# A fused graph-attention and expert-routing block on one core: an expert tile's transposed rows copied on ScalarE, the norms' small sums on GpSimd, new engine orders

## The reference

```python
x = x + gnn(layernorm(x), adj)      # 4-head graph attention, masked softmax over 128 neighbours
h = layernorm(x)
h1 = h + causal_attention(rmsnorm(h, ln1_w)) @ wo.T        # 4 heads, 2 key/value heads, rotary
flat = rmsnorm(h1, ln2_w)
probs = softmax(flat @ router_w.T);  tp, ti = top_k(probs, 2)    # 8 experts
out = sum over e of weights[:, e] * ((silu(flat @ w1[e].T) * (flat @ w3[e].T)) @ w2[e].T)   # hidden 341
x = x + h1 + out
```

## Time and profile before

| | before |
|---|---|
| median of 3 executions | 1731.81 us (1727.41 to 1735.3) |
| the profiled execution | 1738.94 us, span 1737.1 |
| PE busy | 1524.0 us, 88% of the span |
| DVE busy | 1409.4 us, 81% |
| ACT busy | 1052.2 us, 61% |
| POOL busy | 913.5 us, 53% |
| granted PE clock, mean | 0.976 |

### The profile page before, as it was taken

How to read it: one execution, slowest core, us unless ns; L and a number is a source line. 1 busy time by engine, 2 the same in 40 slices (tenths; PEclk the granted TensorE clock), 3 DMA queues, 4 the chain that set the end, 5 groups by cost and what they waited for, 6 DMA issues and landing times. The chain is left out here.

```text
span 1737.1 us, 40737 instructions
## 1 busy us (share of the span) xinstructions
PE 1524.0 (88%) x10930; PEld 1122.8 (65%) x10930; DVE 1409.4 (81%) x4725; ACT 1052.2 (61%) x4092; POOL 913.5 (53%) x720
## 2 busy tenths in 40 slices
PE   4778998999899899999999999999999899987672
PEld 3555666776676667766667676777676666765451
DVE  4678888898889888988898888888889888875441
ACT  3576666766666667666666666666666666653221
POOL 2134565555555555556656655556555555555433
PEclk8899999999999999999999999999999999999897
...
DMA packets 141737, 79.08 MB, mean 46 GB/s; under 512 B 31909, under 2 KB 137165, under 8 KB 141261
## 3 DMA queue, kind: packets, MB, share of 16 engines
...
...
## 5 line engine op out<-in xcount | busy, mean ns | idle before, releaser
L452 POOL DMA_INDIRECT out<-ys,xt x264 | 430.5, 1631 | 511.5 <-DMA out<-ys,xt 383.4
L436 POOL DMA_INDIRECT routed<-fx,slot x256 | 257.9, 1007 | 199.1 <-DVE slot L845 131.7
L1132 PE MATMUL bank<-w_s,hsT 128*128 (+1 forms) x1584 | 230.3, 282 | 17.2 <-ACT hsT L599 16.5
L1132 PEld LDWEIGHTS bank<-w_s,hsT 128*128 128x128 f32 (+1 forms) x1584 | 202.8, 192 | 65.7 <-issue 60.9
L592 ACT ACTIVATE sg<-bank 128x341 f32<-128x341 f32 x264 | 120.6, 457 | 165.0 <-PE bank L1111 149.3
L541 ACT ACTIVATE p<-ub,nm 128x128 f32<-128x128 f32 x512 | 198.0, 390 | 34.3 <-DVE nm L767 33.7
L1111 PE MATMUL bank<-w_s,xT 128*128 x528 | 203.0, 466 | 6.6 <-DVE xT L907 3.0
L598 ACT ACTIVATE hsT<-bank 128x256 f32<-128x256 f32 x264 | 101.2, 384 | 165.7 <-PE bank L1125 141.1
L913 DVE SCALAR_TENSOR_TENSOR hg<-sg,bank 128x341 f32<-128x341 f32 x264 | 133.7, 507 | 82.8 <-ACT sg L592 77.1
L1115 PE MATMUL bank<-w_s,xT 128*128 x528 | 197.0, 455 | 0.1
L1125 PE MATMUL bank<-ident,hu 128*128 128x128 f32 (+1 forms) x792 | 137.6, 283 | 54.1 <-DVE ys L931 43.0
...
## 6 DMA issues: line engine op xcount, KB each, us to landing
xt<-routed SPq DMA_DIRECT2D x264, 65.0 KB
...
out<-ys,xt POOLq DMA_INDIRECT x264
...
```

The lines of the kernel that those rows point to most:

```text
L436: pool.indirect_dma_start(routed, bass.IndirectOffsetOnAxis(slot[p][:, i:i + 1], 0), fx[i // GB][p][:, i % GB, :], None).then_inc(S[f"sc{p ...
L452: pool.indirect_dma_start(out_rows, bass.IndirectOffsetOnAxis(xt[r][:, C:C + 1].bitcast(I32), 0), ys[r][:], None, compute_op=ALU.add, **bo ...
L1132: last = pe.matmul(y_p[:, 0:C], hsT[r % 2][0:n, c, :], w2_s[0:n, bass.ds(e, 1), c, :].rearrange("p a c -> p (a c)"), start=c == 0, stop=c ...
```

## The change

Three things are changed.

1. The copy of the transposed tile from PSUM to xT is done by ACT in place of DVE, with the same waits and the same semaphore. The step E.x moves from the lists of DVE to those of ACT.
2. The small sums in front of the three roots are done by POOL, directly before its root. DVE's step T.ms is gone; N.nx and M.na end on DVE with the statistics.
3. ORDER is laid out anew for PE, DVE, ACT, POOL and SP. In FILLING and DRAINING E.x and T.ms leave DVE's lists, E.x joins ACT's, and the rest keeps its sequence, PE's included.

The ORDER table and the moved steps:

```diff
 ORDER = {
     "pe": """
-        F.x.7 T.yT F.t.6 G.xn F.u.7 G.h F.d.6 A.hN G.p1.0 A.q E.x.0 F.t.7 G.p1.1 E.u.0 T.wo F.d.7 E.x.1 A.k G.o1.0 E.u.1 E.t.0 G.p1.2 E.x.2
-        E.d.0 G.v1.0 E.u.2 E.t.1 T.f A.s2.0 E.d.1 E.x.3 T.lg E.t.2 E.u.3 G.o1.1 E.d.2 A.s2.1 T.rank G.v1.1 E.x.4 A.o2.0 G.o1.2 E.u.4 G.p1.3
-        G.v1.2 E.t.3 E.x.5 A.s2.2 E.d.3 A.v2.0 E.t.4 E.u.5 G.o1.3 A.o2.1 A.s2.3 A.v2.1 G.v1.3 A.o2.2 E.x.6 G.ot E.d.4 A.v2.2 E.u.6 E.t.5
+        F.x.7 T.yT G.xn F.u.7 G.h F.t.6 A.hN G.p1.0 F.d.6 A.q E.x.0 T.wo F.t.7 E.u.0 G.o1.0 F.d.7 E.x.1 G.p1.1 E.u.1 E.t.0 A.k G.v1.0 E.d.0
+        G.p1.2 E.x.2 T.f E.t.1 E.u.2 A.s2.0 E.d.1 E.x.3 T.lg E.t.2 G.o1.1 E.u.3 A.o2.0 E.d.2 A.s2.1 T.rank G.v1.1 A.v2.0 E.x.4 G.o1.2 E.u.4
+        G.p1.3 G.v1.2 E.t.3 E.x.5 A.s2.2 E.d.3 E.u.5 A.o2.1 E.t.4 G.o1.3 A.s2.3 A.v2.1 G.v1.3 A.o2.2 G.ot E.d.4 E.x.6 A.v2.2 E.t.5 E.u.6
         A.o2.3 E.d.5 A.v2.3""".split(),
     "dve": """
-        G.xn F.x.7 A.hN T.yT F.d.6 F.u.7 F.g.7 G.p1.0 E.x.0 A.q E.u.0 T.wo E.g.0 E.x.1 F.d.7 G.p1.1 T.ms E.u.1 A.kk E.g.1 E.x.2 T.f E.d.0
-        G.p1.2 E.u.2 A.s2.0 E.d.1 E.g.2 E.x.3 T.lg E.u.3 E.d.2 E.g.3 E.x.4 T.rank A.s2.1 E.u.4 E.g.4 G.p1.3 E.x.5 A.s2.2 E.d.3 T.tab N.nx
-        E.u.5 A.s2.3 E.x.6 G.ot E.d.4 E.g.5 A.rb E.u.6 M.na E.g.6 E.d.5""".split(),
+        G.xn T.yT A.hN F.u.7 F.g.7 G.p1.0 F.d.6 A.q E.u.0 T.wo E.g.0 F.d.7 G.p1.1 E.u.1 T.f E.g.1 A.kk E.d.0 G.p1.2 E.u.2 E.g.2 A.s2.0 E.d.1
+        T.lg E.d.2 E.u.3 E.g.3 A.s2.1 T.rank E.u.4 E.g.4 G.p1.3 A.s2.2 N.nx E.d.3 T.tab A.s2.3 E.u.5 G.ot E.g.5 E.d.4 A.rb M.na E.u.6 E.d.5
+        E.g.6""".split(),
     "act": """
-        G.xn F.u.7 F.t.6 G.h A.hN F.t.7 E.u.0 A.v G.p1.0 T.wo E.u.1 G.o1.0 E.t.0 G.p1.1 A.kk E.u.2 E.t.1 T.f G.v1.0 A.s2.0 E.t.2 E.u.3 T.lg
-        G.p1.2 G.o1.1 G.v1.1 G.o1.2 E.u.4 A.s2.1 A.o2.0 E.t.3 T.rank G.v1.2 G.p1.3 A.v2.0 A.s2.2 E.u.5 A.o2.1 G.o1.3 A.v2.1 G.v1.3 E.t.4
-        A.o2.2 A.s2.3 A.v2.2 E.u.6 E.t.5 A.o2.3 A.v2.3""".split(),
+        F.x.7 G.xn F.u.7 G.h F.t.6 A.hN E.x.0 G.p1.0 F.t.7 E.u.0 A.v G.o1.0 E.x.1 T.wo E.u.1 E.t.0 A.kk G.p1.1 E.x.2 E.t.1 E.u.2 T.f E.x.3
+        G.v1.0 A.s2.0 E.t.2 G.o1.1 T.lg A.o2.0 E.u.3 G.p1.2 G.v1.1 E.x.4 E.u.4 G.o1.2 A.s2.1 E.t.3 E.x.5 A.v2.0 G.v1.2 G.p1.3 A.s2.2 E.u.5
+        A.o2.1 G.o1.3 A.v2.1 G.v1.3 E.t.4 A.o2.2 A.s2.3 T.rank E.x.6 A.v2.2 E.t.5 E.u.6 A.o2.3 A.v2.3""".split(),
     "pool": """
-        F.s.6 F.s.7 T.ms E.s.0 E.s.1 T.sc.0 E.s.2 T.sc.1 E.s.3 T.sc.2 T.sc.3 N.nx T.sc.4 G.ot T.sc.5 T.sc.6 M.na T.sc.7 E.s.4 E.s.5""".split(),
+        F.s.6 T.ms F.s.7 E.s.0 E.s.1 E.s.2 T.sc.0 T.sc.1 T.sc.2 N.nx T.sc.3 T.sc.4 E.s.3 G.ot T.sc.5 T.sc.6 M.na T.sc.7 E.s.4 E.s.5""".split(),
     "sp": """
-        F.l.7 E.l.0 E.l.1 E.l.2 E.l.3 E.l.4 E.l.5 N.nx T.f E.l.6""".split(),
+        F.l.7 E.l.0 E.l.1 E.l.2 E.l.3 E.l.4 N.nx E.l.5 T.f E.l.6""".split(),
 }
...
     # POOL, step ms_ (nx and na get theirs in the same way)
+                    pool.wait_ge(S["sq"], t + 1)
+                    pool.tensor_scalar(ve_t[:], ms[:], 1.0 / C, EPS_RMS, ALU.mult, ALU.add).then_inc(S["ve_t"], 1)
                     pool.wait_ge(S["ve_t"], t + 1)
                     pool.tensor_tensor(r3[:], ve_t[:], half[:, 0, :], ALU.pow).then_inc(S["r3"], 1)
...
     # ACT
+                def out_x(r):
+                    act.wait_ge(S["xtr"], k8 + r + 1)
+                    if late(k8, 1) or r >= 2:
+                        act.wait_ge(S["h3"], k8 + r - 1)
+                    act.activation(xT[r % 2][:], x_p[:, 0:128], ACT.Copy).then_inc(S["xT"], 1)
...
     # DVE
-                def out_x(r):
-                    dve.wait_ge(S["xtr"], k8 + r + 1)
-                    if late(k8, 1) or r >= 2:
-                        dve.wait_ge(S["h3"], k8 + r - 1)
-                    dve.tensor_copy(xT[r % 2][:], x_p[:, 0:128]).then_inc(S["xT"], 1)
```

More of the change, by code:

```diff
@@ L61 @@
     "dve": """
[L62 to L64 removed]
+        G.xn A.hN F.u.7 F.d.6 F.g.7 N.nx T.yT G.p1.0 A.q E.u.0 T.wo E.g.0 F.d.7 G.p1.1 E.u.1 A.kk E.g.1 E.d.0 T.f A.s2.0 G.p1.2 E.u.2 E.d.1
+        E.g.2 T.lg E.u.3 A.s2.1 E.g.3 T.rank E.d.2 E.u.4 G.p1.3 E.g.4 A.s2.2 E.d.3 T.tab E.u.5 A.s2.3 E.g.5 G.ot E.d.4 A.rb E.u.6 E.g.6 M.na
+        E.d.5""".split(),
     "act": """
[L66 to L68 removed]
+        F.x.7 F.t.6 F.u.7 G.xn G.h A.hN G.p1.0 E.x.0 E.u.0 F.t.7 A.v T.wo E.t.0 E.x.1 E.u.1 A.kk G.o1.0 G.p1.1 E.t.1 E.x.2 E.u.2 T.f G.v1.0
+        A.s2.0 E.x.3 E.u.3 T.lg G.o1.1 E.t.2 G.p1.2 G.v1.1 A.o2.0 E.x.4 A.s2.1 E.u.4 G.o1.2 E.t.3 E.x.5 A.v2.0 G.v1.2 G.p1.3 A.s2.2 A.o2.1
+        G.o1.3 E.u.5 E.t.4 A.v2.1 G.v1.3 A.s2.3 A.o2.2 E.x.6 E.u.6 A.v2.2 E.t.5 A.o2.3 T.rank A.v2.3""".split(),
     "pool": """
@@ L401, in nx @@
                         pool.wait_ge(S["xn"], 4 * n)
+                    pool.wait_ge(S["mv_g"], 4 * n + 4)
+                    pool.tensor_scalar(ve_g[:], mv_g[:, :, 1], EPS_LN, None, ALU.add).then_inc(S["ve_g"], 1)
                     pool.wait_ge(S["ve_g"], n + 1)
@@ L405, in na @@
                 def na():
-                    pool.wait_ge(S["va"], a + 1)
+                    pool.wait_ge(S["mv_a"], 4 * a + 4)
                     if late(a, 1):
                         pool.wait_ge(S["hN"], 4 * a)
+                    v = mv_a[:, :, 1]
+                    pool.tensor_scalar(va[:, 0, :], v, EPS_LN, None, ALU.add)
+                    pool.tensor_scalar(va[:, 1, :], v, 1.0 + EPS_RMS, EPS_RMS * EPS_LN, ALU.mult, ALU.add).then_inc(S["va"], 1)
+                    pool.wait_ge(S["va"], a + 1)
                     pool.tensor_tensor(rr[:], va[:], half[:], ALU.pow).then_inc(S["norm_a"], 1)
@@ L601, in steps @@
                 return {"xn": xn_, "hN": hN_, "h": h, "v": v, "kk": kk_, "wo": wo_, "f": f_, "lg": lg_, "rank": rank, "v1": values1, "v2": values2,
-                        "p1": exp1, "s2": exp2, "o1": out1, "o2": out2, "u": gate, "t": out_h}
+                        "p1": exp1, "s2": exp2, "o1": out1, "o2": out2, "x": out_x, "u": gate, "t": out_h}
             act.wait_ge(S["ready"], 2)
@@ L706, in wo_ @@
                                       z[p][:].rearrange("p b c -> p (b c)"), ALU.add).then_inc(S["x2"], 1)
-                def ms_():
-                    dve.wait_ge(S["sq"], t + 1)
-                    if late(t, 1):
-                        dve.wait_ge(S["r3"], t)
-                    dve.tensor_scalar(ve_t[:], ms[:], 1.0 / C, EPS_RMS, ALU.mult, ALU.add).then_inc(S["ve_t"], 1)
                 def f_():
@@ L931, in weigh @@
                         dve.tensor_scalar(ys[r][:], y_p[:, 0:C], xt[r][:, C + 1:C + 2], None, ALU.mult).then_inc(S["ys"], 1)
-                return {"nx": nx, "na": na, "xn": xn_, "hN": hN_, "wo": wo_, "ms": ms_, "f": f_, "q": q_, "kk": kk_, "lg": route1,
-                        "rank": route2, "tab": tab, "p1": scores1, "s2": max2, "ot": ot, "rb": rb, "yT": yT_, "x": out_x, "u": gate, "g": gated, "d": weigh}
+                return {"nx": nx, "na": na, "xn": xn_, "hN": hN_, "wo": wo_, "f": f_, "q": q_, "kk": kk_, "lg": route1,
+                        "rank": route2, "tab": tab, "p1": scores1, "s2": max2, "ot": ot, "rb": rb, "yT": yT_, "u": gate, "g": gated, "d": weigh}
             steps(-1, 1)["nx"]()
```

18 lines of the change are left out of this document (6 added, 12 removed).

## The result

The changed kernel takes 1715.24 us (median of 4, 1713.48 to 1718.73) where the kernel before took 1731.32 (4 runs, 1727.41 to 1735.3) in the same comparison: a ratio of 0.9906 with a 95% interval of 0.9883 to 0.9929. It is 16 us faster, where 39 were forecast. The profiled execution took 1714.39 us with a span of 1712.6, against 1738.94 and 1737.1.

A forecast was written before the change was run, and what follows sets the result against it. PE was taken as nearest bound, about 46.2 us of a 49.56 us body. Per body 1.6 + 0.33 - 0.25 - 0.3 = 1.4, taken as 1.6; 24.5 x 1.6 = 39 us less, 1693 against the median; range 1670 to 1730.

The forecast's parts named there:

- Bodies of 48.0 us: 24.5 x 1.6 = 39 us less: Sum over the ORDER bodies: each 1.6 us shorter, taken from 1.4 to 2.5, giving 39 us in all.
- the ogT wait: PE's output transposes wait for ACT's last copy, about 1.0 us per body, unexplained; left in, gain about 2.5 if it goes.
- the 46.19 that was read as the floor: PE's busy time per 49.56 us body: no order of the same matmuls could go under about 46.2 us.
- The wait of 1.6 us at E.t.1: PE waits for tile 0's weighing on DVE, behind scalings awaiting a late POOL root; 1.6 us per body would go.
- Fill and drain: I cost both at nothing, bounds -8 and +4: Both ends of the kernel: PE's order unchanged, the drain set by POOL's landing chain; cost nothing, bounds -8 and +4 us.
- rival C: Slower because xT is late on ACT: 0.4 us PE wait per copy, 1.6 us per body, 1771 us; chance 0.09.
- What changes is the queue that it stands in: xT copy: behind score operations on DVE, about 2.1 us; behind four exponentials on ACT, 1.56 us; cost nothing except two places.
- Rival D: Slower by small sums on POOL at 1.04 us each: POOL's floor up 3, body 1 us longer, 1756 us; chance 0.05.
- Rival A: POOL becomes the bound, bodies end at 48.9 us: only 16 us less, 1716 us; chance 0.17.
- POOL's floor: Shortest body POOL allows, from scatter landings plus its other work: 46.6 to 49.2 us, where it was about 45.6.
- Rival B, nothing gained,: The 1.6 us per body turn up again at another in-order wait: 1732 us; chance 0.10.
- Rival E: The unexplained wait for ACT's last attention output copy goes too: 2.5 us per body, 61 less, 1671 us; chance 0.07.

The follow-up runs named there:

- chip M: Chip of a later comparison: the unmodified changed kernel took 1721.25 us there, ratio 0.9888 to the kernel before, which took 1742.02 us.
- chip N: Chip of the last comparison, both kernels unmodified: the changed kernel took 1756.06 us, ratio 1.0084 to the kernel before.
- moves_only: Kernel before with xT copied on ACT, each E.x right ahead of its E.u, and small sums on POOL, but the old ORDER: 1897.8 us, ratio 1.0928.
- ends_dve: Changed kernel with the copy of xT back on DVE in FILLING and DRAINING only: 1705.37 us, ratio 0.982 to the kernel before.
- order_wide: Changed kernel with ORDER serving bodies 4 to 31, so also 4, 5 and 31: 1702.99 us on chip K, 1703.95 on chip M.
- xt_alone: Kernel before with only the xT copy moved to ACT, each E.x right ahead of its E.u: 1900.36 us, ratio 1.094.
- sums_alone: Kernel before with only the four small sums moved to POOL, old order otherwise: 1779.08 us, ratio 1.0229.
- pool_plus_again: Changed kernel with one more unread 1.67 us power on POOL in each T.ms, run beside the changed kernel on chip M: 1730.38 us, ratio 0.9937.
- before_x6_behind: Kernel before with only E.x.6 moved behind E.d.4 on PE and behind G.ot on DVE, in ORDER: 1734.1 us, ratio 0.9968.

## Why the prediction came out as it did

The direction and the range held; the time was 22 us too low. Of the 23 us that the gain fell short of 39, the two ends are 12 and the steady part of the profiled pair 2.6; the other 8 lie between that pair and the medians and are in no term of the sum.

**"Bodies of 48.0 us: 24.5 x 1.6 = 39 us less".** In the profiled pair the steady part gave 36.6 us in 24 bodies, 1.53 each, near the term. But the two profiles are of different kinds, so part of that agreement is luck. By the medians, with the ends at the 12 us that they cost in the pair, I estimate 28 us or 1.2 a body for the first comparison (16 and 12) and 33 us or 1.4 a body on chip M (21 and 12); on N it is nothing. (The body before is 49.25 us by the starts of og; the 49.56 that the windows were cut at was the length of one body.) Its composition was not as forecast. PE's listed waits of 0.2 us and more sum to 73.3 us before (the eight lines from 300 to 1450 us) and to 59.4 after, 0.6 us of a body less, and the ogT wait alone, which the forecast had left in, is 0.8 less; the new waits take back much of what went. The rest is PE's own busy time. Here are the whole steady part before, cut at the starts of og, and the windows of one body after (sum and mean of 24):

```profile
297.07:1479.03 1181.96, 1101.99 (x8114) 819.38 (x8114) 1045.12 (x3504) 776.96 (x3050) 675.32 (x529) 1.00 0.25 46
sum 1145.30, PE 1083.42 PEld 821.48 DVE 1003.45 ACT 813.04 POOL 699.26; mean PE 45.14 PEld 34.23 DVE 41.81 ACT 33.88 POOL 29.14
```

PE is busy 45.14 us a body after and 45.92 before, with the same matmuls and both at a granted clock of 1.00. So the 46.19 that was read as the floor was none: 0.27 of it came of windows a little longer than a body, and 0.78 went when the waits moved. DVE is at 41.8 (forecast 40.9), ACT at 33.9 (34.7).

**The wait of 1.6 us at E.t.1** went, by the chain that was walked, on N as well as in the profile after. The wait for ogT (19.0 us), which I had left in, is gone too in that profile, whose kind of profile doesn't show it in moves_only either. Unforecast on the other side are hN's transposes (0.4 a body: DVE waits 0.7 a body for the root rr, which POOL now begins behind its own sums) and a wait of 0.5 at E.t.5. The normalized rows wait 0.8 a body instead of 0.4: 0.4 lost for a forecast 0.3.

**"Fill and drain: I cost both at nothing, bounds -8 and +4".** This is the step that failed. It measured +13.8 us in bodies 4, 5, 6 and 31 of the profiled pair, and -1.6 in the rest of the ends: 12 in all, three times the upper bound. The pair on chip N, both of one kind, has 12.4 us more in the same four bodies. The argument was that PE's order in both tables is as before. But the lists of ACT are not: E.x stands right ahead of E.u in most places, and where exponentials are ahead of both, PE waits for the copy, up to 2.0 us. That is rival C, which I had priced for ORDER, where E.x was placed with care, and never for the tables where it wasn't. ends_dve and order_wide (1705 and 1703 us on chip K) show what the change is worth without it: with the copy's place mended the ends are back at 45.8 to 50.2 us a body, and on chip M order_wide is 17 us under the changed kernel.

**"What changes is the queue that it stands in".** Right in kind, and far too cheap as a price of a bad place: rival C had 0.4 us per copy and 1771 us; moves_only and xt_alone have 140 us and more in 102 or 103 waits, 1.4 us each, and 1898 and 1900 us. What such waits do to the granted clock (0.97 in the steady part) was in no term either.

**Part 2.** The small sums measured 0.25, 0.33, 0.22 and 0.20 us, 1.0 us per body where 1.2 was taken. From the groups of after:

```profile
L606 ACT ACTIVATE xT<-bank 128x128 f32<-128x128 f32 x264 | 73.5, 278 | 149.3 <-PE bank L1094 148.3
```

is the copy on ACT at 278 ns, forecast 271. The rule that was weighed there, of the Trainium skill (GPSIMD Engine Reference, "Performance versus the Vector engine"), about twice as long on GpSimd, rests in that section on an add of two tensors with 2048 elements; taken over to these sums, which have one input tensor, it is an estimate of 0.32 us each against 0.161 on DVE. Measured are 0.20 to 0.33, 1.2 to 2 times. Rival D falls, since it needed 1.04 each. But the lengths are not harmless in every place: in sums_alone, with sums as short, they stand on the path to two roots and the kernel is 43 us slower.

**Rival A** falls by pool_plus_again. POOL's floor was worked out as 46.6 to 49.2; a body of 47.72 excludes the upper part, above that.

**Rival B, nothing gained,** had 0.10. On chip N it is what the steady part does: the 1.6 us at E.t.1 are gone and PE waits 36.6 us for ys in 39 waits, up from 30.1, by the late og above. **Rival E** took the unexplained wait to go with the new order. It is gone in the profile after, but in moves_only it is gone with the old order of PE; before_x6_behind speaks against the one place that was tried on L.
